# The edge round on VectorE in a graph layer: order of its products, of the Newton steps and of the shift

## The reference, cut to what matters

```python
h = jnp.maximum(_layernorm(x, axis=-1), 0.0)
s, v = h[:, :64], h[:, 64:].reshape(N, 32, 3)
skip_s, skip_v = s @ W_skip0, einsum('nmi,mk->nki', v, W_skip1)
s, v = s @ W_nl0, einsum('nmi,mk->nki', v, W_nl1)
sh1 = SQRT3 * edge_attr / norm(edge_attr)
w = relu(edge_feature @ W_fc1) @ W_fc2            # split into w0..w4
xs, xv = s[dst], v[dst]
tp = concat([w0 * xs,
             w3 * (einsum('emi,ei->em', xv, sh1) * INV_SQRT3),
             (w1 * xs)[:, :, None] * sh1[:, None, :],
             w2[:, :, None] * xv,
             w4[:, :, None] * (cross(xv, sh1[:, None, :]) * INV_SQRT2)])
agg = segment_sum(tp, src, num_segments=N) / 32.0
out_s = agg[:, :96] @ W_out_s + skip_s
out_v = einsum('nmi,mk->nki', agg_v, W_out_v) + skip_v
x = x + concat([silu(out_s[:, :64]), sigmoid(out_s[:, 64:96])[:, :, None] * out_v])
```

## Time and profile before

| | |
|---|---|
| median of 3 runs | 1174.71 us |
| the profiled execution | 1174.41 us |
| its span in the trace | 1172.6 us |
| TensorE matmul busy | 1098.8 us (94%) |
| VectorE busy | 983.7 us (84%) |
| ScalarE busy | 856.2 us (73%) |
| GpSimd busy | 683.3 us (58%) |
| mean granted TensorE clock | 0.982 of full |

### The profile page before, as it was taken

One profiled execution on the slowest core, in us unless ns is written; L12 is line 12 of the kernel. 1 busy time (PEld: TensorE's weight loads), 2 busy tenths in 40 slices (PEclk: granted clock), 3 DMA queues, 4 the chain that ended last, 5 costly groups with the idle time before them and its releaser, 6 DMA issues.

```text
span 1172.6 us, 29282 instructions
## 1 busy us (share of the span) xinstructions
PE 1098.8 (94%) x8847; PEld 921.6 (79%) x8847; DVE 983.7 (84%) x3571; ACT 856.2 (73%) x2069; POOL 683.3 (58%) x860
## 2 busy tenths in 40 slices
PE   6889899999999999995999999999999999999996
PEld 5567688888888887885888888888878888878885
DVE  9999888888888889865688888888888888888874
ACT  0401477777777777774888899988899888888984
POOL 6777777777777777756144554445554445544460
PEclk9999899999999999995999999999999999999998
DMA  9999454544444675433677777777777777777763
GB/s 344 403 403 402 162 138 135 137 131 134 132 139 139 179 253 144 136 109 114 221 276 280 274 265 278 285 277 280 282 254 285 278 281 281 256 279 280 282 208 111
DMA packets 108459, 271.12 MB, mean 231 GB/s; under 512 B 13573, under 2 KB 51751, under 8 KB 108364
## 3 DMA queue, kind: packets, MB, share of 16 engines
q1 hardware_dynamic: 87852, 233.20, 56.5%
q0 software_dynamic: 19200, 36.48, 10.4%
q10 hardware_dynamic: 1312, 0.29, 0.1%
HBM read 126.91 MB, written 143.01 MB: 230 GB/s over the span
## 4 chain that ended last, share of the span: by engine, by line
PE 66%; DVE 19%; issue 7%; ACT 4%; DMA 2%; POOL 1%; DVEq 0%; SPq 0%; ACTq 0%; POOLq 0%
PE bank L1449 16%; PE bank L1462 9%; PE bank L1441 8%; PE bank L1453 5%; PE bank L1378 5%; PE bank L1313 4%; PE bank L1281 3%; PE bank L1391 3%; DVE ob L1031 3%; PE bank L1395 3%; PE bank L1363 2%; DVE n_stat L940 2%; PE bank L1407 2%; PE bank L1393 2%; DVE bin_hot L626 2%
## 5 line engine op out<-in xcount | busy, mean ns | idle before, releaser
L1230 ACT ACTIVATE nn<-xb,n_bias,n_rstd 128x160 f32<-128x160 f32 x784 | 346.3, 528 | 46.6 <-POOL n_bias L567 35.9
L512 POOL DMA_INDIRECT slots<-msg,sidx x200 | 204.2, 1021 | 84.3 <-issue 53.9
L940 DVE BATCH_NORM_STATS2 n_stat<-xb 128x6 f32<-128x160 f32 x784 | 196.1, 312 | 25.6 <-DMA xb<-x 25.0
L1031 DVE SCALAR_TENSOR_TENSOR ob<-sg,bank 128x128 f32<-128x128 f32 x588 | 131.8, 279 | 73.1 <-ACT ob L1245 71.5
L1462 PE MATMUL bank<-mg,hot 64*128 64x192 f32 x1568 | 171.8, 338 | 7.4 <-DVE hot L1016 7.4
L544 POOL TENSOR_TENSOR n_sum<-n_stat 128x32 f32<-128x32 f32 x24 | 6.9, 288 | 281.2 <-DVE n_stat L940 281.2
L561 POOL TENSOR_TENSOR n_rstd<-n_sum,neg_half 128x8 f32<-128x8 f32 x94 | 160.1, 1703 | 5.7 <-issue 2.9
L1449 PE MATMUL bank<-fwd,nt 128*128 128x160 f32 x784 | 144.6, 307 | 15.5 <-DVE ob L1031 13.9
L502 POOL DMA_INDIRECT xg<-x,dst_i x136 | 132.4, 974 | 44.5 <-issue 43.6
L1237 ACT ACTIVATE nt<-bank 128x640 f32<-128x640 f32 x196 | 137.7, 703 | 17.7 <-PE bank L1442 13.7
L1038 DVE TENSOR_TENSOR ob<-ob,xb 128x1280 f32<-128x1280 f32 x98 | 147.1, 1501 | 3.4
(11 more groups left out here) (191 smaller groups left out, 2571.5 us busy)
## 6 DMA issues: line engine op xcount, KB each, us to landing
xb<-x SPq DMA_DIRECT2D x97, 640.0 KB, 5.2
out_dram<-ob SPq DMA_DIRECT2D x97, 640.0 KB, 3.3
slots<-blank SPq DMA_DIRECT2D x14, 2744.0 KB, 30.5
mg<-slots SPq DMA_DIRECT2D x98, 392.0 KB, 4.0
messages<-msg SPq DMA_DIRECT2D x50, 382.8 KB
ef<-edge_feat_t SPq DMA_DIRECT2D x50, 125.0 KB
slots<-msg,sidx POOLq DMA_INDIRECT x200, 3.8
xg<-x,dst_i POOLq DMA_INDIRECT x136, 6.7
```

The source lines that it names most:

```text
L512: pool.indirect_dma_start(slots[:, :], bass.IndirectOffsetOnAxis(ap=sidx[:, m:m + 1], axis=0), msg[:, c, t, 0:MW], None).then_inc(e_sc[c], 16)
L940: done = dve.bn_stats(n_stat[:, u // U, u % U * G + g, :], xb[:, u, g, :])
L1031: last = dve.scalar_tensor_tensor(out=o[:, :, S + V * j:S + V * j + V], in0=sg[:, h, :, :], scalar=1.0, in1=z[:, :, part], op0=ALU.add, op ...
L1230: last = act.activation(nn[:, u % 2, h, spread_of(g % 4)], xb[:, u, g, order_of(g % 4)], ACT.Relu, bias=n_bias[:, u // U, c:c + 1], scale= ...
```

## The change

VectorE's order in `round_e` is written anew. `xvh` goes ahead of `hu` and of the squares; it no longer waits for `e_wsb` and `e_tt`, which are now waited for ahead of the first product that needs them (L903's). The first halves of the cross product stand ahead of the variance and the message add, the two `dot` sums come later. The reciprocal, the Newton step and the shift are no longer done in the odd round but at the end of the even one, between the four statistics of group q + 4. On ScalarE `root_e` goes ahead of the second half of `norm_e`. No instruction is added or taken away.

```diff
                 def round_e(q):
-                    p, c, m = q - 1, (q + 1) % 2, q // 2 + 1
-                    root, spread = q % 2 == 1 and within(q + 1), q % 2 == 0 and within(q + 3)
-                    r = q - 3
-
-                    if root:
-                        guess_e(m)
+                    p, c, m, r = q - 1, (q + 1) % 2, q // 2 + 1, q - 3
+                    spread = q % 2 == 0 and within(q + 3)
                     if spread:
                         spread_e(m)
+                    if within(p):
+                        ...
+                        dve.wait_ge(e_xs, p + 1)
+                        wait(dve, e_tp, p)
+                        dve.tensor_tensor(xvh[:], ...).then_inc(e_dot, 1)
+                    if spread:
+                        squares_e(m)
                     if within(r):
                         ...
                         dve.tensor_tensor(hu[:], ...).then_inc(e_hu, 1)
-                    if root:
-                        newton_a(m)
-                    if spread:
-                        squares_e(m)
                     if within(p):
-                        ...
-                        dve.wait_ge(e_wsb, p + 1)
-                        dve.wait_ge(e_xs, p + 1)
-                        wait(dve, e_tp, p)
-                        wait(dve, e_tt, GE * (p - 1))
-                        dve.tensor_tensor(xvh[:], ...).then_inc(e_dot, 1)
-                    if root:
-                        newton_b(m)
+                        dve.tensor_tensor(cr_a[:, :, 0:2, :], ...)
+                        dve.tensor_tensor(cr_a[:, :, 2, :], ...)
                     if spread:
                         variance_e(m)
                     if within(r):
                         dve.wait_ge(e_hu, r + 1)
                         dve.tensor_tensor(v, v, hu[:], ALU.add)
                         dve.tensor_copy(msg[...], place_of[...]).then_inc(e_fix, 1)
-                    if root:
-                        newton_c(m)
                     if within(p):
-                        dve.tensor_tensor(cr_a[:, :, 0:2, :], ...)
-                        dve.tensor_tensor(cr_a[:, :, 2, :], ...)
-                        dve.wait_ge(e_dot, 3 * p + 1)
-                        dve.tensor_tensor(dot[:, 0, :, :], ...).then_inc(e_dot, 1)
                         dve.tensor_tensor(cr_b[:, :, 0, :], ...)
                         dve.tensor_tensor(cr_b[:, :, 1:3, :], ...).then_inc(e_cross, 1)
-                        dve.wait_ge(e_dot, 3 * p + 2)
-                        dve.tensor_tensor(dot[:, 1, :, :], ...).then_inc(e_dot, 1)
-                    if root:
-                        shift_e(m)
-                    if within(p):
+                        dve.wait_ge(e_dot, 3 * p + 1)
+                        dve.tensor_tensor(dot[:, 0, :, :], ...).then_inc(e_dot, 1)
+                        dve.wait_ge(e_wsb, p + 1)
+                        wait(dve, e_tt, GE * (p - 1))
                         dve.tensor_tensor(tp[:, c, :, V:V + 2 * S]..., ALU.mult)
+                        dve.wait_ge(e_dot, 3 * p + 2)
+                        dve.tensor_tensor(dot[:, 1, :, :], ...).then_inc(e_dot, 1)
                         ...
+                    if spread:
+                        guess_e(m)
                     if within(q + 4):
-                        stats_e(q + 4)
+                        stats_e(q + 4, range(0, 1))
+                    if spread:
+                        newton_a(m)
+                    ...
+                    if spread:
+                        shift_e(m)
 ...
                     put(q - 2, 0)
+                    if q % 2 == 0 and within(q + 3):
+                        root_e(q // 2 + 1)
                     if within(q + 1):
                         norm_e(q + 1, range(2, 4))
-                    if q % 2 == 0 and within(q + 3):
-                        root_e(q // 2 + 1)
                     take(3)
```

More of the change, by code:

```diff
@@ L845, in round_e @@
                 def round_e(q):
-                    p, c, m = q - 1, (q + 1) % 2, q // 2 + 1
-                    root, spread = q % 2 == 1 and within(q + 1), q % 2 == 0 and within(q + 3)
-                    r = q - 3
-                    if root:
-                        guess_e(m)
+                    p, c, m, r = q - 1, (q + 1) % 2, q // 2 + 1, q - 3
+                    spread = q % 2 == 0 and within(q + 3)
                     if spread:
                         spread_e(m)
+                    if within(p):
+                        rows = f_x if p == 0 else p_x
+                        row_s, row_v = rows[:, :, 0:S], rows[:, :, S:F].rearrange("p t (i k) -> p t i k", i=3)
+                        w = w_sb[:, c, :, :]
+                        h = hat[:, p * GE:p * GE + GE, :]
+                        parts = tp[:, c, :, V + 2 * S:TU].rearrange("p t (i k) -> p t i k", i=3)
+                        dve.wait_ge(e_xs, p + 1)
+                        wait(dve, e_tp, p)
+                        dve.tensor_tensor(xvh[:], h[:, :, 0:3].unsqueeze(3).to_broadcast((ET, GE, 3, V)), row_v, ALU.mult
+                                          ).then_inc(e_dot, 1)
+                    if spread:
+                        squares_e(m)
                     if within(r):
@@ L861, in round_e @@
                                           ALU.mult).then_inc(e_hu, 1)
-                    if root:
-                        newton_a(m)
-                    if spread:
-                        squares_e(m)
                     if within(p):
[L867 to L871, removed]
-                        dve.wait_ge(e_wsb, p + 1)
-                        dve.wait_ge(e_xs, p + 1)
-                        wait(dve, e_tp, p)
-                        wait(dve, e_tt, GE * (p - 1))
-                        dve.tensor_tensor(xvh[:], h[:, :, 0:3].unsqueeze(3).to_broadcast((ET, GE, 3, V)), row_v, ALU.mult
-                                          ).then_inc(e_dot, 1)
-                    if root:
-                        newton_b(m)
+                        dve.tensor_tensor(cr_a[:, :, 0:2, :], row_v[:, :, 1:3, :],
+                                          h[:, :, 2:4].unsqueeze(3).to_broadcast((ET, GE, 2, V)), ALU.mult)
+                        dve.tensor_tensor(cr_a[:, :, 2, :], row_v[:, :, 0, :],
+                                          h[:, :, 1:2].to_broadcast((ET, GE, V)), ALU.mult)
                     if spread:
@@ L885, in round_e @@
                         dve.tensor_copy(msg[0:ET, r % MR, :, LOCAL:NODE + 1], place_of[:, r * GE:r * GE + GE, :]).then_inc(e_fix, 1)
-                    if root:
-                        newton_c(m)
                     if within(p):
[L889 to L892, removed]
-                        dve.wait_ge(e_dot, 3 * p + 1)
-                        dve.tensor_tensor(dot[:, 0, :, :], xvh[:, :, 0, :], xvh[:, :, 1, :], ALU.add).then_inc(e_dot, 1)
                         dve.tensor_tensor(cr_b[:, :, 0, :], row_v[:, :, 2, :], h[:, :, 1:2].to_broadcast((ET, GE, V)), ALU.mult)
@@ L897, in round_e @@
                                           h[:, :, 2:4].unsqueeze(3).to_broadcast((ET, GE, 2, V)), ALU.mult).then_inc(e_cross, 1)
-                        dve.wait_ge(e_dot, 3 * p + 2)
-                        dve.tensor_tensor(dot[:, 1, :, :], dot[:, 0, :, :], xvh[:, :, 2, :], ALU.add).then_inc(e_dot, 1)
-                    if root:
-                        shift_e(m)
-                    if within(p):
+                        dve.wait_ge(e_dot, 3 * p + 1)
+                        dve.tensor_tensor(dot[:, 0, :, :], xvh[:, :, 0, :], xvh[:, :, 1, :], ALU.add).then_inc(e_dot, 1)
+                        dve.wait_ge(e_wsb, p + 1)
+                        wait(dve, e_tt, GE * (p - 1))
                         dve.tensor_tensor(tp[:, c, :, V:V + 2 * S].rearrange("p t (j k) -> p t j k", j=2),
@@ L905, in round_e @@
                                           row_s.unsqueeze(2).to_broadcast((ET, GE, 2, S)), ALU.mult)
+                        dve.wait_ge(e_dot, 3 * p + 2)
+                        dve.tensor_tensor(dot[:, 1, :, :], dot[:, 0, :, :], xvh[:, :, 2, :], ALU.add).then_inc(e_dot, 1)
                         dve.wait_ge(e_cross, p + 1)
@@ L917, in round_e @@
                                           ).then_inc(e_tp, 1)
+                    if spread:
+                        guess_e(m)
                     if within(q + 4):
-                        stats_e(q + 4)
+                        stats_e(q + 4, range(0, 1))
+                    if spread:
+                        newton_a(m)
+                    if within(q + 4):
+                        stats_e(q + 4, range(1, 2))
+                    if spread:
+                        newton_b(m)
+                    if within(q + 4):
+                        stats_e(q + 4, range(2, 3))
+                    if spread:
+                        newton_c(m)
+                    if within(q + 4):
+                        stats_e(q + 4, range(3, 4))
+                    if spread:
+                        shift_e(m)
```

## The result

| | before | after |
|---|---|---|
| median of six runs each, same chip | 1174.28 us (1171.95 to 1176.09) | 1167.37 us (1163.01 to 1170.37) |
| ratio, 95% interval | | 0.9936 [0.9908, 0.9964] |
| profiled execution, its span | 1174.41, 1172.6 us | 1170.37, 1168.5 us |
| GpSimd busy | 683.3 us | 691.3 us |
| mean granted TensorE clock | 0.982 | 0.973 |

The change is faster by 6.9 us; 14.6 were forecast.

What follows compares the result with a forecast made beforehand. TensorE was taken to bound the edge rounds, with ScalarE's wait for the shift costing 0.93 us per pair. 21 pairs x (16.29 - 15.56) = 15.3, less 0.7 at the ends, gave 14.6 us less: 1159.8 us, range 1153.5 to 1166.5.

Steps and rivals of the forecast that it cites:

- What bounds the kernel: Edge rounds: TensorE has almost no idle time, except 0.93 us per pair lost through ScalarE's wait for `e_bias`.
- part 1: Newton step and shift at the even round's end: the 0.93 us per pair go, no new stall at the root.
- the sum: Whole execution: 21 pairs gain 15.3 us, start +0.3, rounds 38 to 41 -0.5, end -0.5: 14.6 us less.
- Part 2: GpSimd's scatters and gathers, released later: it stops waiting and falls behind slightly; cost 0, up to 1 us once.
- Part 3: Longer VectorE chain to TensorE's transposes: GpSimd holding the second square costs 0.20 us per pair, bounds 0 to 0.8.
- Part 4: The ends: start gains 0.3 us, rounds 38 to 41 lose 0.5, the chain to the last scatter loses 0.5.
- GpSimd becomes the pace: Rival in the edge rounds: GpSimd sets 15.72 us per pair, 11.3 us gained, 1163.1 us; chance 0.10.
- the deep ring: Argument against GpSimd setting the pace: the ring of 8 messages is 60 us deep.
- The mean holds: Rival: GpSimd holds both two-port VectorE instructions' followers, mean case, pair of 16.05 us, 1170.1 us; chance 0.10.
- No hold passes on: Rival: the even chain fits its 0.16 us slack, pair of 15.36 us, 18.8 us gained, 1155.6 us; chance 0.17.
- Holds at their worst phase: Rival, before the last product: GpSimd holds VectorE 0.9 us each, pair of 17.48 us, 1200 us; chance 0.05.

Runs made afterwards that it cites:

- Newton-only kernel: Kernel before with only the reciprocal, Newton step, shift and root moved, VectorE's products in the old order: 1157.35 us, ratio 0.9827.
- the repeat: The changed kernel run again unaltered, on the same chip as other follow-up kernels: 1163.67 us, ratio 0.9903 to the kernel before.
- The extra product of the experiment: Newton-only kernel plus one unused VectorE sum per round behind `crx`, both inputs in SBUF: 1156.75 us, ratio 0.9863 to the kernel before.
- the kernel with the root behind: Newton-only kernel, but with ScalarE's root left behind the second half of the normalisation: 1156.0 us, ratio 0.9859 to the kernel before.
- the PSUM kernel: Changed kernel with one input of `hu`, the message add and `crx` taken from PSUM, for timing only: 1157.82 us, ratio 0.985 to the kernel before.

## Why the prediction was right and where it failed

- **What bounds the kernel, and part 1** were right. The wait for `e_bias` is gone, the odd round went from 8.61 to 7.69 us, and the Newton-only kernel shows that this part alone carries the whole gain and more than the whole change keeps. No stall came at the root, but its place wasn't free, as the sum had it: it is the 0.10 us by which the even round of every kernel with the root ahead (7.78) exceeds 7.68.
- **Part 2 failed, and its cost is about the whole miss, 14.6 - 6.9 = 7.7 us.** Moving the gathers alone takes the ratio from 0.9936, or 0.9903 in the repeat, to 0.9853, which is 9.7 or 5.9 us. It put GpSimd at "15.72 per pair", the last gather "near 473", and its cost at "0, up to 1 us". That it "stops waiting and falls behind" was right. But the 15.72 took GpSimd's durations from the trace of before as given. In the new order they grow by holds (1020 to 1047 ns, 1016 to 1071): 16.2 us per pair, and the last gather came at 481.58. The difference, (16.2 - 15.72) x 18 = 8.6 us, is just what separates 481.58 from 473. Its data was wanted near 477 by the prediction's own step. The lead of 15.75 us at round 43 fell to 8.35 by waits and to 3.51 with the low clock behind them; a cost of 12.2 us in this profiled execution, the slowest of the six, and 7.2 in the other one (16.3 to 9.1). With the gathers moved ahead and all else as changed the ratio is 0.9853, or 15.2 us less than the kernel before with the same edit, where the sum without this cost had 14.6.
- **That nearness is partly luck.** With the gathers moved the rounds are 18.9 us ahead at round 48, where the sum's terms give 15.3 + 0.3 - 0.5 = 15.1, and its last scatter is only 15.0 us ahead (534.38 against 549.36): GpSimd, held, took back 4.0 us where the prediction had 0.5 for the end.
- **Part 3**: the term was mis-sized. I took 0.20 us per pair for holds that pass on, and the runs show none: in all 19 rounds between 150 and 440 us `hu` starts 0.15 us behind the first square (L652), in the eight where the second, L653, is held (0.38 to 0.41 us) as in the others. The pair takes 7.78 + 7.69 = 15.47, and the 0.11 above 15.36 is the root's place. L653's mean is 264 ns where I expected 300 to 500. I had looked for holds in one direction only, GpSimd's on VectorE, and priced that; the costly ones are VectorE's on GpSimd.
- **Part 4**: the start gave 0.36 us (X of round 2 136.76 against 137.12), 0.3 forecast. Rounds 38 to 41 took 33.12 against 33.32, no loss where I had 0.5. The end can't be read apart from the low clock in the changed kernel.
- **The rivals.** "GpSimd becomes the pace" (1163.1) had the right engine, but the wrong course: GpSimd didn't set the pace of the rounds, they ran on at 15.47 on the data gathered ahead until it ran out. "Against: the deep ring" was an argument about messages. The gathers stand in the same queue: at the end they are issued 11 groups ahead of the one scattered, which is four ahead of the one whose statistics are taken in that round, and that lead wasn't divided by the rate at which it was consumed. The mean holds (1170.1) lie nearest to the measured 1167.37, by chance, as their pair of 16.05 was 15.47. "No hold passes on" was right about VectorE. Holds at their worst phase (1200 us) didn't occur on VectorE.

Why the new order and not the old one has starts in the products is worked out here and not shown by a run of its own. Undisturbed, GpSimd starts every 1.29 us, and six of them (7.74) nearly fill a round of 7.69 to 7.78, so that the starts keep their places in the round. In the changed order the two-SBUF stretches are, from X = 299.25 on, `hu` at 0.47 to 1.02, the add at 1.47 to 2.02, `dot` and `crx` at 3.34 to 4.09, the last two `tp` products at 4.48 to 5.25. Taken modulo 1.29, and each less the last 0.13, they cover all places but about 0.1 us. With `hu` ahead of `xvh` and `dot` apart from `crx` there are gaps of some 0.3 us, and GpSimd, pushed by each hold, comes to rest in one: in the rows of the Newton-only kernel above it starts at 300.02, 0.09 ahead of the add's end, and at 302.58, 0.16 ahead of the end of `crx`. The extra product of the experiment didn't close that gap: the starts that fell in it settled at its last 0.11 us.

## What to carry to other kernels

An engine that has just lost its waits has to be priced again, with durations that may grow, and its backlog at the last moment somebody asks for its product counts, not its mean rate: (its pace - the rounds' pace) x the number of rounds, against the lead. When half of a change removes the wait that the profile shows, try that half alone; the other half here took away about half of the gain (0.9903 and 0.9936 against 0.9827). And stalls of a few us on TensorE can cost twice, once as themselves and once by the clock behind them: 1.7, 2.0 and 2.5 us of idle time were followed by 17.1 us at the lower level in one execution of the changed kernel and by 6.8 in another, while a single wait of 3.35 us in the kernel with the root behind had no low clock behind it.

## What the runs showed of the hardware

A DMA_INDIRECT instruction of GpSimd takes 0.97 us and its next starts 0.30 us later. If it starts while VectorE runs a product with both inputs in SBUF, it ends later by the rest of that product less about 0.1 us (1.31 to 1.57 in the rows above). It isn't held by a product with an input in PSUM (0.99), nor by a two-SBUF product that starts behind it (0.97). In the other direction little shows: of the changed kernel's `hu` products and message adds between 150 and 430 us the longest takes 0.62 us, where 0.55 is usual. The Trainium skill, "SBUF — State Buffer", the section "Who interferes with whom", says that a VectorE instruction with two SBUF inputs contends with a GpSimd instruction that reads SBUF, and that issue order decides who is blocked; the PSUM kernel's 991 ns against 1047 agree. The same section of the Trainium skill has it that a plain tensor-tensor wasn't seen to stall such DMAs; here GpSimd's DMA instructions took 1.263 us instead of 0.987 when they started in one with both inputs in SBUF, and the measurement decides.
